# Token stage of a transformer layer in another order: keys turned in one go, query halves apart, values in 32 products

## The chip, the cores and the metric

The kernel runs on one core of one Trainium2 chip. The metric is the device time of one execution in microseconds; for a kernel several executions are timed and their median is given. Beside them one execution is profiled, and all rows of the trace come from that one.

## The reference, cut to what matters

Input `x` has 8192 rows (tokens) of 512 numbers. All is float32. The weights are drawn at random.

```
n   = layernorm(x)
cq, ckv = n @ Wc + bc, n @ Wckv + bckv               # 128 columns each
q   = [cq @ Wcq + bcq | cq @ Wqr + bqr]              # 16 heads of 32 + 16 columns
k   = [ckv @ Wck + bck | n @ Wkr + bkr]              # 16 heads of 32 + 16 columns
v   = ckv @ Wv + bv                                  # 16 heads of 32 columns
s   = q[token] @ k[token].T * scale                  # 16 x 16 for each token: heads against heads
x1  = x + layernorm(softmax(s) @ v -> 512 columns, @ Wo + bo)
xf  = layernorm(x1)
out = x1 + layernorm(experts(xf) + shared_mlp(xf))   # 64 experts, 6 chosen for a token
```

The attention is inside a token: its 16 heads attend to each other. So for 128 tokens there are 128 little products of 16 x 48 x 16 (scores) and of 16 x 16 x 32 (values).

## The kernel before, in words

The kernel has two stages, one after the other. The first, `token_pipeline`, goes through 64 tiles of 128 tokens and does everything up to the hidden layer of the shared MLP and the choice of experts. The second, `experts_and_norm`, runs the 64 experts, adds the results to the rows and normalises. Only the first is touched.

The token stage is a software pipeline written out by hand. Each engine has a function `iteration(i, par)`; in iteration `i` tile `i` is at its first step (latents), tile `i-1` gets queries, keys and values, `i-2` its scores, probabilities and value products, `i-3` the product with `wo` and the first residual, `i-4` the second layernorm's statistics, `i-5` the shared MLP's first product and the gate, `i-6` its stores. The order of work on an engine is the order of the `if active(...)` blocks in its function; engines wait for each other by counting semaphores, and a wait stops all that stands behind it on the same engine. The middle iterations run in a loop on all engines, two iterations in one turn of the loop.

The order of TensorE in one iteration: transposes of `xf` into `s0` (half of the score banks), transposes of the queries (`turn(q, ...)`) into banks b3 and b7, the first part of the latents' product into b5 (`high`, 8 matmuls of 512 columns), transposes of half of the keys into b2, the second part of the latents (`low`, 4 matmuls), transposes of the other half of the keys into b3, `v` into b6, the two query halves into b4 and b5, the first half of the MLP's product (`wgu`, 12 matmuls of 416 columns) into b7, scores, transposes of `oin`, the second half of `wgu` into b4, `high` of `wo` into b7, transposes of the first half of the probabilities, `low` of `wo`, transposes of the second half, key product `wck` into b6, transposes of the latents, `rank` (one small product, L611), and the value products (L623) into b4 and b5.

Every float32 product of dense weights is split in three: high part by high part and high part by low part (`high`, L502/L503 and L473/L474), and low part by high part (`low`, L508 and L477). ScalarE (ACT) writes the high parts, VectorE (DVE) subtracts to make the low parts (`low_part`, L767). Small products (scores, values) are plain float32; a plain float32 matmul appears in the trace as two MATMUL instructions.

Scores and values go by blocks of four tokens. `spread` on ACT copies the transposed queries and keys out of PSUM, 48 partitions x 256 elements at a time, 8 copies for queries and 8 for keys (L644, tiles qT and kT), into 64-row halves of qT and kT. The scores are then 32 products with 48 rows and 64 columns of weights, and 64 moving columns. For the values, `vbd` holds the values of a tile with (half, token of the block, head) on the partitions, and the value step makes for each of 8 column blocks four products: two halves of the partitions (64 rows) times two column groups, each with 32 moving columns:

```
last = nc.tensor.matmul(pv_ps[h][64 * g:64 * g + 64, n * DH:n * DH + DH],
                        probT[64 * h:64 * h + 64, n, 64 * g:64 * g + 64],
                        vbd[64 * h:64 * h + 64, par, 2 * n + g], start=True, stop=True)
```

The two partition halves go to two banks (`pv_ps`: halves of b4 and b5), and DVE scales each bank into `o` (L904). `o` then travels through memory to change its layout: SP (the DMA queue's engine) stores it with four DMAs to `o_scratch` and, when those have landed, loads it back with four DMAs into `oin`, which TensorE transposes about half an iteration later. `v` goes through `v_scratch` into `vbd` in the same manner.

DVE's order in an iteration: statistics of x (`st<-xin`), low part of `xfT`, statistics of x1, `lat` and the rotary part of `k` (L817, L821, both read b5), `v` (L827), the two query halves (L832), `xf` (L762), the gated unit's first half (L776 to L783, after ACT's tanh L682), the softmax steps (L845 to L858), low part of `oT`, gate steps, the gated unit's second half, sums, `y` (L891), `k` (L894), statistics of y, `o` (L904, twice), low parts of `latT` and `xT`, `yn`.

Ahead of the pipeline the weights are loaded in parts, staged in tiles that the pipeline does not use yet (wo's four parts in `vbd`), and split (`split`) on ACT and DVE in iterations -1, 0 and 1.

Of the kernel before, what the change touches and what calls it, by code (L numbers as in the profile page):

```python
# [35 lines left out]
ALU = mybir.AluOpType  # L36
# [71 lines left out]
def settle(eng):  # L108

    eng.nop(nofuse=True)  # L110
# [47 lines left out]
def token_pipeline(nc, x, xt, cst, w_lat, b_lat, w_q, b_q, w_ck, b_ck, w_v, b_v, w_o, b_o, w_gu,  # L158
                   x1_d, xf_d, h_d, acc_d, v_d, o_d, rank_d, wlat, wq, wck, wv, load_expert, c, tri, all_ranks, ranks_in):
    ctx = ExitStack()  # L160
    with ctx:
# [14 lines left out]
        pv_ps = (b4[:, 0:256], b5[:, 0:256])  # L176
# [21 lines left out]
        v_all = sb("vbd", [P, 4 * D])  # L198
        vbd = v_all[:, 0:2 * D].rearrange("p (a n d) -> p a n d", a=2, d=DH)
# [22 lines left out]
        rstd = [sb(f"rstd{n}", [P, 1 if n else 2]) for n in range(3)]  # L222
        smax4 = sb("smax4", [P, NBLK, B4])
# [19 lines left out]
        vs = v_all[:]  # L243
# [14 lines left out]
        latent_bias_in = sem("latent_bias_in")  # L258
# [39 lines left out]
        a_kT = count("a_kT", 8)  # L298
# [19 lines left out]
        d_pv = count("d_pv", 2)  # L318
# [33 lines left out]
        def _(sp):  # L352
# [6 lines left out]
            for n, (stage, _, _, src) in enumerate(parts):  # L359
                if n in SPLIT_BEFORE:  # L360
                    sp.wait_ge(part_lo, SPLIT_BEFORE[n])
                sp.dma_start(stage, src).then_inc(part_in[n], 16)
                if n == KD - 1:
                    sp.dma_start(blat[:], b_lat.partition_broadcast(P)).then_inc(latent_bias_in, 16)
                    load_x(1, 1)
# [5 lines left out]
            def iteration(i, par):  # L371
# [54 lines left out]
                if isinstance(i, int) and i == 1:  # L426
                    sp.wait_ge(part_lo, KD + 3 + KD)
                if active(i - 1):
# [8 lines left out]
                    for b in range(2):  # L437
                        sp.dma_start(vbd[64 * b:64 * b + 64, 1 - par], src[b]).then_inc(v_in[1 - par].sem, 16)
# [21 lines left out]
        def _(pe):  # L460
# [57 lines left out]
            def iteration(i, par):  # L518
                latents = b5, [xT[:, :, n, :] for n in range(KD)], [wlat[:, :, n, :] for n in range(KD)]
                normed = [xfT[:, :, n, :] for n in range(KD)]  # L520
# [36 lines left out]
                if active(i - 1):  # L557
                    pe.wait_ge(d_pv.sem, d_pv.at(i - 3))
                    for n, b in enumerate((b4, b5)):
                        if n == 1:  # L560
                            pe.wait_ge(d_lat.sem, d_lat.at(i))
                        product(b[:, 0:8 * DQ], [latT[:, 1 - par, :, 0, :]], [wq[:, :, 0, n * 8 * DQ:(n + 1) * 8 * DQ]],
                                d_latT, i - 1, pe_q)
                if active(i - 5):
# [11 lines left out]
                if active(i - 3):  # L576
                    pe.wait_ge(o_in.sem, o_in.at(i - 3))
                    pe.wait_ge(a_kT.sem, a_kT.at(i - 2))
                    transposes(b3, [oin[:, n * P:(n + 1) * P] for n in range(KD)], pe_oT)
# [18 lines left out]
                if active(i - 2):  # L598
                    pe.wait_ge(a_exp.sem, a_exp.at(i - 2, 2))
                    transposes(s1, [pr[:, n * P:(n + 1) * P] for n in range(4, 8)], pe_pT)  # L600
# [3 lines left out]
                if active(i):  # L604
                    pe.wait_ge(d_lat.sem, d_lat.at(i))
                    pe.wait_ge(a_kT.sem, a_kT.at(i - 2, 4))
                    transposes(b2, [lat[:, n * P:(n + 1) * P] for n in range(2)], pe_latT)
                if active(i - 5):
# [4 lines left out]
                if active(i - 2):  # L613
                    pe.wait_ge(a_pT.sem, a_pT.at(i - 2))
                    pe.wait_ge(d_q.sem, d_q.at(i - 1))
                    pe.wait_ge(d_h.sem, d_h.at(i - 5))
                    pe.wait_ge(v_in[par].sem, v_in[par].at(i - 2))
                    settle(pe)
                    for n in range(8):
                        for b in range(2):  # L620
                            for g in range(2):
                                h = (b + g) % 2
                                last = nc.tensor.matmul(pv_ps[h][64 * g:64 * g + 64, n * DH:n * DH + DH],  # L623
                                                        probT[64 * h:64 * h + 64, n, 64 * g:64 * g + 64],
                                                        vbd[64 * h:64 * h + 64, par, 2 * n + g],
                                                        start=True, stop=True)
                    last.then_inc(pe_pv.sem, 1)
# [4 lines left out]
        def _(act):  # L632
# [13 lines left out]
            def iteration(i, par):  # L646
                def spread(dst, src, done, n):

                    for a in range(2):
# [22 lines left out]
                if active(i - 2):  # L672
                    act.wait_ge(pe_kT.sem, pe_kT.at(i - 2, 1))
                    by_token = kT.rearrange("p (c t) (m a) -> p a m c t", t=B4, a=2)
# [54 lines left out]
        def _(dve):  # L729
# [59 lines left out]

            def iteration(i, par):  # L790
# [6 lines left out]
                if active(i - 4):  # L797
                    dve.wait_ge(g_x1.sem, g_x1.at(i - 4))
                    stats(2, x1[:], i - 4)
# [651 lines left out]
```

## Time and profile before

| | us |
|---|---|
| median of 3 runs | 1968.72 (1955.16 to 1973.68) |
| profiled execution, its own time | 1969.8 |
| its span, first to last instruction | 1967.8 |
| PE busy in the span | 1804.6 (92%) |
| DVE busy | 1458.7 (74%) |
| ACT busy | 1039.1 (53%) |
| POOL busy | 548.1 (28%) |

The span is the time between the first and the last instruction of the core; the execution's own time is a little longer. PE is TensorE's matmul side, PEld its weight loads, which run beside the matmuls. A busy share over the whole span mixes the token stage (to about 1,290 us) with the expert stage. Times of a row are the start from the span's start and the duration; the difference of two starts on one engine is what an instruction costs in a packed stream, since consecutive instructions overlap.

### The profile page before, as it was taken

The numbers are of one execution on the slowest core, as the hardware profiler recorded it, in microseconds if no ns is written. First come the engines' busy times: TensorE is split into PE (matmuls) and PEld (weight loads), VectorE is DVE, ScalarE is ACT, GpSimd is POOL, SyncE is SP. The second block draws the span as 40 slices with busy tenths as digits, with TensorE's granted clock in tenths as the row PEclk, the third lists the DMA queues.
The fourth block names the chain that finished last, engine by engine and source line by source line (L and its number), as shares of the span: only waits on it lengthen the run. The fifth ranks groups of instructions, "written<-read, shape, count | busy, mean of one in ns | idle before, by whom it ended". The sixth has DMA issues, their size and how long they took to land. (4 is left out here: it accounts for less than half of the span.)

```text
span 1967.8 us, 53720 instructions
## 1 busy us (share of the span) xinstructions
PE 1804.6 (92%) x16329; PEld 1410.4 (72%) x16329; DVE 1458.7 (74%) x3876; ACT 1039.1 (53%) x2257; POOL 548.1 (28%) x772
## 2 busy tenths in 40 slices
PE   5899999999999999999999999966799999978886
PEld 3688888888888888888888888753455555556564
DVE  6688888888888888888888888844344444439897
ACT  4576667676767676766666666621233323223333
POOL 1021212121212121212121212111344444437777
PEclk8799999999999999999999999977899999999999
DMA  6355565656565656565566656476999999979994
GB/s 221 82 146 161 151 170 149 170 149 171 148 170 148 169 149 170 153 165 154 165 154 164 163 156 171 119 191 222 293 306 307 288 293 299 290 233 387 403 385 162
DMA packets 549277, 400.85 MB, mean 204 GB/s; under 512 B 424873, under 2 KB 433193, under 8 KB 549161
## 3 DMA queue, kind: packets, MB, share of 16 engines
q1 hardware_dynamic: 528672, 341.77, 59.3%
q0 software_dynamic: 14336, 35.66, 7.7%
q10 hardware_dynamic: 6208, 22.68, 3.1%
q8 instruction: 30, 0.49, 0.1%
q14 instruction: 31, 0.25, 0.0%
HBM read 249.24 MB, written 150.63 MB: 203 GB/s over the span
## 5 line engine op out<-in xcount | busy, mean ns | idle before, releaser
L935 POOL TENSOR_SCALAR ve<-mv 128x1 f32<-128x1 f32 x192 | 43.1, 225 | 986.1 <-DVE mv L758 986.1
L644 ACT COPY kT<-bank 48x256 f32<-48x256 f32 x512 | 307.9, 601 | 12.6
L1140 PE MATMUL e_gu<-w,xgT 128*128 128x384 f32 x512 | 187.3, 510 | 20.7 <-issue 11.1
L473 PE MATMUL bank<-wgu,xfT 128*128 128x416 f32 x512 | 188.9, 369 | 6.5 <-ACT xfT L644 5.6
L644 ACT COPY qT<-bank 48x256 f32<-48x256 f32 x512 | 187.7, 367 | 12.6 <-PE bank L466 1.6
L474 PE MATMUL bank<-wgu,xfT 128*128 128x416 f32 x512 | 182.8, 357 | 0.0
L1301 DVE SCALAR_TENSOR_TENSOR tanh<-tanh,e_gu 128x192 f32<-128x192 f32 x64 | 22.6, 354 | 174.9 <-ACT tanh L1227 174.9
L1140 PEld LDWEIGHTS e_gu<-w,xgT 128*128 128x128 f32 x512 | 94.2, 194 | 80.3 <-issue 20.3
L1384 POOL DMA_INDIRECT acc_scratch<-eo,sidx x64 | 101.5, 1586 | 128.8 <-ACT eo L1223 112.0
L644 ACT COPY probT<-score_ps 128x512 f32<-128x512 f32 x128 | 75.2, 588 | 112.0 <-PE score_ps L466 112.0
L1163 PE MATMUL e_ps<-w,hidT 96*128 96x512 f32 x256 | 127.0, 618 | 1.6 <-ACT hidT L1215 0.9
L776 DVE SCALAR_TENSOR_TENSOR th<-th,bank 128x176 f32<-128x176 f32 (+1 forms) x128 | 44.7, 349 | 108.2 <-ACT th L682 105.5
L477 PE MATMUL bank<-wgu,xfT 128*128 128x416 f32 x512 | 118.1, 353 | 0.0
L502 PE MATMUL bank<-wlat,xT 128*128 128x512 f32 x256 | 108.2, 423 | 6.4 <-DVE wlat L749 5.0
L937 POOL TENSOR_TENSOR rstd<-ve,mhalf 128x1 f32<-128x1 f32 x192 | 108.8, 566 | 16.0
L1215 ACT COPY hidT<-e_ps 96x256 f32<-96x256 f32 x64 | 23.5, 367 | 167.7 <-PE e_ps L1147 167.7
L950 POOL TENSOR_TENSOR x<-yn,xres 128x512 f32<-128x512 f32 x64 | 82.3, 1285 | 91.5 <-DVE yn L762 91.5
L1244 ACT ACTIVATE f_acc<-f_acc,f_shift,f_rstd 128x512 f32<-128x512 f32 x64 | 48.7, 808 | 107.1 <-POOL f_shift L1405 107.1
L473 PEld LDWEIGHTS bank<-wgu,xfT 128*128 128x128 f32 x512 | 98.9, 193 | 8.3 <-ACT xfT L644 6.4
L1413 POOL TENSOR_TENSOR f_res<-f_acc,f_res 128x512 f32<-128x512 f32 x64 | 94.6, 1500 | 33.9 <-ACT f_acc L1244 18.2
L502 PE MATMUL bank<-wo,oT 128*128 128x512 f32 x256 | 102.7, 401 | 1.4 <-ACT oT L644 1.4
L503 PE MATMUL bank<-wlat,xT 128*128 128x512 f32 x256 | 103.2, 403 | 0.0
(178 smaller groups left out, 4789.2 us busy)
## 6 DMA issues: line engine op xcount, KB each, us to landing
w<-w_eg SPq DMA_DIRECT2D x60, 768.0 KB, 6.5
acc_scratch<-zero SPq DMA_DIRECT2D x130, 256.0 KB, 4.0
w<-w_ed SPq DMA_DIRECT2D x60, 384.0 KB, 10.5
xf_scratch<-xf SPq DMA_DIRECT2D x64, 288.0 KB, 2.1
xin<-x SPq DMA_DIRECT2D x64, 256.0 KB, 3.0
x_raw<-xt SPq DMA_DIRECT2D x64, 256.0 KB, 3.3
v_scratch<-v SPq DMA_DIRECT2D x64, 256.0 KB, 3.5
vbd<-v_scratch SPq DMA_DIRECT2D x128, 128.0 KB, 3.2
```

What stands on the lines that cost most here:

```text
L473: nc.tensor.matmul(dst, a[:, 0], b[:, 0], start=(n == 0), stop=False)
L474: nc.tensor.matmul(dst, a[:, 0], b[:, 1], start=False, stop=False)
L477: last = nc.tensor.matmul(dst, a[:, 1], b[:, 0], start=False, stop=(n == len(lhs) - 1))
L502: nc.tensor.matmul(dst, a[:, 0], b[:, 0], start=(n == 0), stop=False)
L503: nc.tensor.matmul(dst, a[:, 0], b[:, 1], start=False, stop=False)
L644: nc.scalar.copy(dst, src).then_inc(done.sem, 1)
L937: nc.gpsimd.tensor_tensor(to, ve[n][:], mhalf[:], ALU.pow).then_inc(g_rstd[n].sem, 1)
L950: nc.gpsimd.tensor_tensor(x1[:], yn[:], xres[:], ALU.add).then_inc(g_x1.sem, 1)
L1140: last = nc.tensor.matmul(gu_ps[par], xgT[:, par, n, :], w1[:, place, n, :], start=(n == 0), stop=(n == KD - 1))
L1163: last = nc.tensor.matmul(out_ps, hidT[:, n, :], w2[0:PI, (place - 1) % NW, n, :], start=(n == 0), stop=(n == 1))
L1384: nc.gpsimd.indirect_dma_start(acc_d[1 - par], bass.IndirectOffsetOnAxis(sidx[:, (place - 1) % NW, :].bitcast(U32), 0), eo[:, (place - 1) ...
L1413: nc.gpsimd.tensor_tensor(r, acc[:, u, n * D:(n + 1) * D], r, ALU.add).then_inc(g_sum.sem, 1)
```

## The change

It reorders the token stage on TensorE and DVE and changes three steps. Nothing of the arithmetic's result changes.

1. TensorE: `low` of the latents stands right behind `high`, and both halves of the keys are transposed one after the other behind it. `high` no longer waits for `o` of the tile before (`d_pv`), because b5 no longer holds value products.
2. TensorE: the second query half (into b5) moves from in front of `wgu`'s first half to behind it, with its wait for `d_lat`. DVE's matching add moves behind the gated unit's first half.
3. TensorE: both halves of the probabilities are transposed one after the other, inside wo's product; `low` of `wo` comes behind them.
4. Values: `vbd` is block diagonal: for each token block and partition half b, the values fill column part b and zeros the other. One product has 128 rows, 64 columns of weights and 64 moving columns; 16 products (32 MATMUL instructions) take the place of 32 (64). All go to b4, and DVE makes `o` in one operation. The zeros are written once, by a memset on GpSimd in iteration 0, behind the split of wo's parts; the DMAs into `vbd` write strided pieces of 32 numbers. The value products stand ahead of `rank`.
5. Keys: ACT makes 6 of the 8 key copies (b3's second partition half is left out), DVE makes the other two (`d_kT`), behind the first query half.
6. DVE: `lat` and the rotary part of `k` move ahead of the statistics of x1 (and, in iteration 0, ahead of the weight splits), `k` moves behind `o`.
7. The latent bias is counted with the other biases: DVE waits for all five in iteration 0.

```
 TensorE
                 if active(i):
                     pe.wait_ge(a_xT.sem, a_xT.at(i))
                     pe.wait_ge(d_q.sem, d_q.at(i - 2))
-                    pe.wait_ge(d_pv.sem, d_pv.at(i - 3))
                     high(*latents)
+                if active(i):
+                    pe.wait_ge(d_xT.sem, d_xT.at(i))
+                    low(*latents, pe_lat)
                 if active(i - 2):
...
                     turn(k[:, par], pe_kT, 0, b2)
-                if active(i):
-                    pe.wait_ge(d_xT.sem, d_xT.at(i))
-                    low(*latents, pe_lat)
                 if active(i - 2):
                     pe.wait_ge(a_qT.sem, a_qT.at(i - 2, 4))
                     turn(k[:, par], pe_kT, 1, b3)
...
                 if active(i - 1):
                     pe.wait_ge(d_pv.sem, d_pv.at(i - 3))
-                    for n, b in enumerate((b4, b5)):
-                        if n == 1:
-                            pe.wait_ge(d_lat.sem, d_lat.at(i))
-                        product(b[:, 0:8 * DQ], ...)
+                    queries(0, b4)
                 if active(i - 5):
...
                     product(b7[:, 0:GU], normed, [wgu[:, :, n, 0:GU] for n in range(KD)], d_xfT, i - 5, pe_gu)
+                if active(i - 1):
+                    pe.wait_ge(d_lat.sem, d_lat.at(i))
+                    queries(1, b5)
                 if active(i - 2):
                     pe.wait_ge(a_kT.sem, a_kT.at(i - 2))
+                    pe.wait_ge(d_kT.sem, d_kT.at(i - 2))
...
                     transposes(s0, [pr[:, n * P:(n + 1) * P] for n in range(4)], pe_pT)
+                if active(i - 2):
+                    pe.wait_ge(a_exp.sem, a_exp.at(i - 2, 2))
+                    transposes(s1, [pr[:, n * P:(n + 1) * P] for n in range(4, 8)], pe_pT)
                 if active(i - 3):
                     pe.wait_ge(d_oT.sem, d_oT.at(i - 3))
                     low(*turned, pe_wo)
...
                     for n in range(8):
-                        for b in range(2):
-                            for g in range(2):
...
+                        for g in range(2):
+                            last = nc.tensor.matmul(b4[64 * g:64 * g + 64, n * 64:n * 64 + 64],
+                                                    probT[:, n, 64 * g:64 * g + 64],
+                                                    vbd[:, par, 2 * n + g].rearrange("p b d -> p (b d)"),
+                                                    start=True, stop=True)
                     last.then_inc(pe_pv.sem, 1)
+                if active(i - 5):
+                    pe.wait_ge(d_r.sem, d_r.at(i - 5, 6))
+                    pe.wait_ge(a_pT.sem, a_pT.at(i - 2))
+                    nc.tensor.matmul(rank_ps, chosen[:], tri[:], start=True, stop=True).then_inc(pe_rank.sem, 1)
 ACT
-                    spread(by_token, b3, a_kT, 1)
+                    spread(by_token, b3, a_kT, 1, (0,))
 DVE (behind the first query half)
+                if active(i - 2):
+                    dve.wait_ge(pe_kT.sem, pe_kT.at(i - 2))
+                    dve.wait_ge(pe_s.sem, pe_s.at(i - 3))
+                    settle(dve)
+                    sv = b3[64:64 + DQ, :].rearrange("p (m r c t) -> p r m c t", m=4, r=2, t=B4)
+                    for half in range(2):
+                        nc.vector.tensor_copy(by_token[64 * half:64 * half + DQ, 1, 4:8], sv[:, half]).then_inc(d_kT.sem, 1)
...
                     nc.vector.tensor_tensor(o[:].rearrange("p (n d) -> p n d", d=DH),
                                             b4[:].rearrange("p (n d) -> p n d", d=DH),
                                             srec[:].unsqueeze(2).broadcast_to([P, NBLK, DH]), ALU.mult).then_inc(d_pv.sem, 1)
 SP
-                        sp.dma_start(vbd[64 * b:64 * b + 64, 1 - par], src[b]).then_inc(v_in[1 - par].sem, 16)
+                        sp.dma_start(vbd[64 * b:64 * b + 64, 1 - par, :, b, :], src[b]).then_inc(v_in[1 - par].sem, 16)
 GpSimd
+                if isinstance(i, int) and i == 0:
+                    pool.wait_ge(part_lo, 11)
+                    nc.gpsimd.memset(vbd[:], 0.0).then_inc(zeroed, 1)
```

## Rows read from the trace of the kernel before

**Rows 1.** The page: busy us, then 40 equal slices in tenths, span.

```profile
PE 1804.6 (92%) x16329; PEld 1410.4 (72%) x16329; DVE 1458.7 (74%) x3876; ACT 1039.1 (53%) x2257; POOL 548.1 (28%) x772
PEclk8799999999999999999999999977899999999999
```

**Rows 2.** Stretch 102 to 1243: us, busy by engine, clock, DMA share, GB/s.

```profile
102.00:1243.00 1141.00, 1118.52 (x12946) 968.98 (x12944) 974.04 (x2497) 760.50 (x1686) 209.26 (x407) 1.00 0.60 159
```

**Rows 3.** Tile `lat`, same stretch: duration ns min/median/max, first and last start.

```profile
L817 DVE SCALAR_TENSOR_TENSOR lat<-bank,rstd,blat x59: 482/483/485, 102.4 to 1242.1; 128x256 f32<-128x256 f32 x59
```

**Rows 4.** Waits, same stretch: who for whom, total us, times, longest us.

```profile
DVE th L776 <- ACT th L682: 95.0, 58, 1.7
...
PEld score_ps L493 <- issue: 21.2, 58, 0.6
PEld bank L473 <- DVE k L821: 17.8, 49, 1.4
...
PEld bank L623 <- issue: 11.0, 54, 0.3
...
PEld bank L466 <- DMA oin<-o_scratch: 6.7, 16, 1.2
```

**Rows 5.** Timeline of PE, 726 to 739: start, duration, line, operation.

```profile
726.77 1.14 PE L623 MATMUL bank<-vbd,probT 64*64 64x32 f32 x64
727.84 0.66 PE L466 MATMUL score_ps<-c,xf 128*128 128x128 f32 x4
...
729.16 0.47 PE L502 MATMUL bank<-wlat,xT 128*128 128x512 f32 x1
729.47 0.40 PE L503 MATMUL bank<-wlat,xT 128*128 128x512 f32 x1
729.70 0.39 PE L502 MATMUL bank<-wlat,xT 128*128 128x512 f32 x1
...
731.10 0.60 PE L466 MATMUL bank<-c,k 128*128 128x128 f32 x4
...
732.47 0.60 PE L466 MATMUL bank<-c,k 128*128 128x128 f32 x4
...
737.28 1.16 PE L493 MATMUL score_ps<-kT,qT 48*64 48x64 f32 x64
738.39 0.66 PE L466 MATMUL bank<-c,oin 128*128 128x128 f32 x4
```

**Rows 6.** Timeline of ACT, same iteration.

```profile
732.14 4.99 ACT L644 COPY kT<-bank 48x256 f32<-48x256 f32 x8
```

**Rows 7.** Groups by shape, 102 to 1243: count, busy us, mean ns, idle before.

```profile
L644 ACT COPY kT<-bank 48x256 f32<-48x256 f32 x468 | 281.8, 602 | 11.5
L644 ACT COPY qT<-bank 48x256 f32<-48x256 f32 x464 | 170.1, 367 | 10.0
```

**Rows 8.** Timeline of DVE, same iteration.

```profile
728.26 0.75 DVE L904 TENSOR_TENSOR o<-bank,srec 128x256 f32<-128x256 f32 x2
...
735.57 0.54 DVE L762 TENSOR_SCALAR xf<-x,mv,rstd 128x512 f32<-128x512 f32 x1
737.71 0.34 DVE L776 SCALAR_TENSOR_TENSOR th<-th,bank 128x176 f32<-128x176 f32 x1 [1.59 <-ACT th L682]
...
745.84 0.68 DVE L894 TENSOR_TENSOR k<-bank,bck 128x512 f32<-128x512 f32 x1
```

**Rows 9.** Timeline of SP's DMA issues, same iteration.

```profile
729.12 2.63 SPq L379 DMA_DIRECT2D o_scratch<-o  x4
...
733.43 2.59 SPq L394 DMA_DIRECT2D oin<-o_scratch  x4
```

**Rows 10.** Tile `oin`, 100 to 1236: from issue to landing.

```profile
DMA to landing us min/median/max: 2.2/2.6/4.2
```

**Rows 11.** Timeline of the start, 17 to 25 us, all engines.

```profile
18.67 0.93 DVE L749 TENSOR_TENSOR wq<-kT,wq 128x768 fp32r<-128x768 f32 x1
...
21.47 1.62 PE L508 MATMUL bank<-wlat,xT 128*128 128x512 f32 x4
...
25.00 0.47 DVE L817 SCALAR_TENSOR_TENSOR lat<-bank,rstd,blat 128x256 f32<-128x256 f32 x1
```

More of the change, by code:

```diff
@@ L297, in token_pipeline @@
         a_qT = count("a_qT", 8)
-        a_kT = count("a_kT", 8)
+        a_kT = count("a_kT", 6)
+        d_kT = count("d_kT", 2)
         a_exp = count("a_exp", 2)
@@ L317, in token_pipeline @@
         d_s = count("d_s", 9)
-        d_pv = count("d_pv", 2)
+        d_pv = count("d_pv")
         d_h = count("d_h", 4)
@@ L519, in iteration, with queries @@
                 latents = b5, [xT[:, :, n, :] for n in range(KD)], [wlat[:, :, n, :] for n in range(KD)]
+                def queries(n, b):
+                    product(b[:, 0:8 * DQ], [latT[:, 1 - par, :, 0, :]], [wq[:, :, 0, n * 8 * DQ:(n + 1) * 8 * DQ]],
+                            d_latT, i - 1, pe_q)
                 normed = [xfT[:, :, n, :] for n in range(KD)]
@@ L607, in iteration @@
                     transposes(b2, [lat[:, n * P:(n + 1) * P] for n in range(2)], pe_latT)
+                if active(i - 2):
+                    pe.wait_ge(a_pT.sem, a_pT.at(i - 2))
+                    pe.wait_ge(d_q.sem, d_q.at(i - 1, 1))
+                    pe.wait_ge(d_h.sem, d_h.at(i - 5))
+                    pe.wait_ge(v_in[par].sem, v_in[par].at(i - 2))
+                    settle(pe)
+                    for n in range(8):
+                        for g in range(2):
[3 more added lines that the diff above has]
+                                                    start=True, stop=True)
+                    last.then_inc(pe_pv.sem, 1)
                 if active(i - 5):
@@ L646, in iteration, with spread @@
             def iteration(i, par):
-                def spread(dst, src, done, n):
-                    for a in range(2):
+                def spread(dst, src, done, n, pair=range(2)):
+                    for a in pair:
                         sv = src[64 * a:64 * a + DQ, :].rearrange("p (m r c t) -> p r m c t", m=4, r=2, t=B4)
@@ L788, in low_x, with queries @@
                 low_part(xT, x_raw[:, 1 - par, :], d_xT)
+            def queries(i, n, b):
+                dve.wait_ge(pe_qT.sem, pe_qT.at(i - 2))
+                dve.wait_ge(pe_q.sem, pe_q.at(i - 1, n + 1))
+                nc.vector.tensor_tensor(q[:, 8 * n:8 * n + 8, 0:DQ], b[:, 0:8 * DQ].rearrange("p (h d) -> p h d", d=DQ),
+                                        bq[:, n * 8 * DQ:(n + 1) * 8 * DQ].rearrange("p (h d) -> p h d", d=DQ),
+                                        ALU.add).then_inc(d_q.sem, 1)
             def iteration(i, par):
@@ L796, in iteration @@
                     low_part(xfT, s0, d_xfT)
[L797 to L806 removed]
                 if isinstance(i, int) and i == 0:
[L808 to L810 removed]
+                    dve.wait_ge(biases_in, 16 * 5)
                 if active(i):
@@ L823, in iteration @@
                                                    ALU.mult, ALU.add).then_inc(d_lat.sem, 1)
+                if active(i - 4):
+                    dve.wait_ge(g_x1.sem, g_x1.at(i - 4))
+                    stats(2, x1[:], i - 4)
+                if isinstance(i, int) and i == -1:
+                    low_x(i, par)
+                    dve.wait_ge(centred, 1)
+                    for n in range(KD):
+                        nc.vector.tensor_tensor(parts[n][0], parts[n][0], b2, ALU.subtract).then_inc(centred, 1)
+                if isinstance(i, int) and i in PART_AT:
+                    split(i)
                 if active(i - 1):
@@ L840, in iteration @@
                     gated(i, par, 0, b7)
+                if active(i - 1):
+                    queries(i, 1, b5)
                 sp4 = score_ps[:].rearrange("p (n t h) -> p n t h", n=NBLK, t=B4)
-                half = [slice(n * NBLK // 2, (n + 1) * NBLK // 2) for n in range(2)]
+                halves = [slice(n * NBLK // 2, (n + 1) * NBLK // 2) for n in range(2)]
                 if active(i - 2):
                     dve.wait_ge(pe_s.sem, pe_s.at(i - 2))
-                    nc.vector.tensor_reduce(smax4[:, half[0]], sp4[:, half[0]], AX.X, ALU.max).then_inc(d_s.sem, 1)
-                    nc.vector.tensor_reduce(smax4[:, half[1]], sp4[:, half[1]], AX.X, ALU.max).then_inc(d_s.sem, 1)
+                    nc.vector.tensor_reduce(smax4[:, halves[0]], sp4[:, halves[0]], AX.X, ALU.max).then_inc(d_s.sem, 1)
+                    nc.vector.tensor_reduce(smax4[:, halves[1]], sp4[:, halves[1]], AX.X, ALU.max).then_inc(d_s.sem, 1)
                     dve.wait_ge(d_s.sem, d_s.at(i - 2, 2))
@@ L857, in iteration @@
                     for n in range(2):
[L858 to L859 removed]
+                        nc.vector.tensor_tensor(prob[:, halves[n]], sp4[:, halves[n]],
+                                                sref[:, halves[n]].unsqueeze(3).broadcast_to([P, NBLK // 2, B4, H]),
                                                 ALU.subtract).then_inc(d_s.sem, 1)
```

69 lines of the change are left out of this document (15 added, 54 removed).

## The prediction

> **What bounds the kernel now.** The page comes first: PE is busy 92% of the span, and its clock is granted in full in nearly every slice between the start and the expert stage [rows 1]. Only the token stage is changed, so the next view is the table by stretches over the even part of it, 102 to 1243 us: PE busy 1118.5 of 1141 us (98%), clock 1.00, DVE 974.0 (85%), ACT 760.5 (67%) [rows 2]. TensorE's stream sets the pace, at full clock; the reader should note DVE's 85%, since the change gives DVE more to do. How long is an iteration? `lat` is made once in each: 59 of them from 102.4 to 1242.1, so 1139.7/58 = 19.65 us [rows 3]. PE being nearly always busy, a gain must come out of packed instructions or out of the small holes. The waits list the holes [rows 4], per iteration: 21.2/58 = 0.37 before the scores, 17.8/58 = 0.31 before the second query half (released by DVE's rotary part of `k`, L821), 0.19 before the values, and 6.7/58 = 0.12 before the transposes of `oin`, where a DMA came late 16 times in 58. DVE itself stands 95.0/58 = 1.64 us waiting for ACT's tanh L682; no other hole of its has that size.
>
> **The change part by part, per iteration.** Prices on PE are differences of starts, since neighbours overlap.
>
> Second query half behind `wgu`: the wait on L821 goes. It is 0.31 us of the weight loads' idle time, some of which a running matmul covers; I take 0.25. What is late next there? `wgu`'s first half now starts about 0.8 us earlier, and needs ACT's query copies, finished when the key copies start at 732.14, while `wgu` would start about 4.9 us after the first key transposes, at 734.0 [rows 5, 6]: no wait.
>
> Start of the scores: the eight key copies on ACT run from 732.14 for 4.99 us to 737.13, and the scores start at 737.28 [rows 5, 6]. So ACT's chain ends exactly where the scores begin. The hole of 0.37 has a part that any change of product kind with several waits seems to cost (0.19 before the values, rows 4); the rest, 0.18, is put down to ACT, and I take 0.15 as gained. With six copies of 0.60 [rows 7] ACT needs 3.7 us. It starts later, since the first keys are turned only behind `low`: that is 4 x 0.23 us + 0.08 behind today's start at 731.10, so 732.1, and ready some 0.6 later at 732.7 [rows 5]; 732.7 + 3.7 = 736.4, against scores that would start at about 736.8. Covered, by 0.4 us.
>
> Merging transposes: after transposes, the first wide product costs 729.47 - 729.16 = 0.31 us where the next costs 729.70 - 729.47 = 0.23 [rows 5]. Each return from transposes to a product costs 0.08; the keys in one go and the probabilities in one go save one each: 0.16. The cost would be that the second half of the probabilities is wanted 0.95 us earlier (4 x 0.23 of `low`). It was 1 us and more ready before PE came; I count nothing, and it is the thinnest of the covers on this side.
>
> Values: 64 MATMULs of 32 columns take 727.84 - 726.77 = 1.07 us, 16.7 ns each. 64 of 64 columns in four tiles (the scores) take 738.39 - 737.28 = 1.11, 17.3 each [rows 5]. Twice the columns cost the same, so it looks like a rate of instructions and not of columns. Now 32 MATMULs of 64 columns with all 128 rows, hence two tiles in place of four. Low end: 32 x 17.3 ns = 0.55 us, if the rate of instructions stays. High end with both column groups at work: each group's pass keeps the 4 x 17.3 = 69 ns that a tile has now, 16 passes: 1.11. If the column groups did not overlap at all: 32 x 69 ns = 2.2. No row has this shape; I take the middle of the first two, 0.85, and gain 0.22. The Trainium skill (TensorEngine Tiling (Array Packing), Available Configurations) lists 64x64 as four tiles and 128x64 as two. By that rule the products lose in tiles what they save in number, the values stay at about 1.1 us, and the iteration saves 0.25 us less; the trace shows only the four-tile form.
>
> `high` without `d_pv`, `rank` behind the values: no row has a wait on the one, and the other is the same instruction elsewhere. Nothing. SP's strided DMA pieces are 128 bytes on the memory side before and after; nothing.
>
> Sum on PE: 0.25 + 0.15 + 0.16 + 0.22 = 0.78, iteration 19.65 - 0.78 = 18.87 us.
>
> **DVE, the engine that receives work.** Its sequence, without the wait for the tanh, fills 19.65 - 1.64 = 18.0 us. Added: two copies of 256 elements. Nearest below is half of `o`, same size out of PSUM, 0.75/2 = 0.38 [rows 8]; above it, ACT pays 0.602 for the scattered key copies where the same count of elements costs 0.367 for queries [rows 7], and by that ratio DVE would pay 0.62. I take 0.42, since DVE's row is the nearer one: 0.84. `o` in one operation should be like `k` (0.68 for 512 elements, rows 8) in place of 0.75: -0.07. Sum 18.0 + 0.84 - 0.07 = 18.8, at the ends 18.7 and 19.2. So DVE's chain comes level with PE. What hides the copies is the hole between `xf` (735.57 + 0.54 = 736.11) and 737.71 [rows 8]: 1.6 us, of which the earlier tanh (about 0.8 us) takes half. The copies stand in front of the gated unit and so of the softmax, with the scores waiting for them on PE. They can start when `v` and the first query half are done, about 1.4 us before 736; both would be over at about 736.4, before the scores at 736.8. `lat` earlier gives the rotary part of `k` a wait for the second key transposes of some 0.3 us, with `v` and all else queued behind it. `k` behind `o` is a loss to nobody: its reader is the next iteration's key transposes, over 4 us later. I charge nothing to PE for these, and keep the ends for the range.
>
> **Start.** DVE's weight splits begin at 18.67 and run packed until `lat` at 25.00, while `low` of the first latents ends at 21.47 + 1.62 = 23.09 [rows 11]. Now `lat` stands ahead of the splits: DVE is idle from 18.67 to 23.1, and the same splits end 4.4 us later, with the low parts of the next tile behind them. I add 4.4 us once. GpSimd's memset has its next user, SP's load of the values, some 10 us later: nothing. The expert stage is not touched.
>
> **The forecast.** About 60 iterations at the steady pace x 0.78 = 46.8 us saved, 4.4 lost: 42.4. From the profiled execution, 1969.8 - 42.4 = 1927 us; that execution is 1.1 us above the median of 1968.72, which changes nothing. With the values at 0.55 the gain is 18 us more (1909), at 1.11 it is 16 less (1943). 1% is 20 us, about what a measurement here can tell from no change.
>
> **The rivals.**
>
> A, DVE becomes the bound. For it: 18.8 of 18.9 us, with `prob`, exp and the transposes in a chain behind it. Against it: DVE has its hole just where the copies go. With copies of 0.62 and the 0.3 us wait, an iteration is about 19.2 to 19.3; saved 0.4 x 60 = 24, less 4.4: 1950.
>
> B, the round trip of `o` through memory decides. Its stores are issued from 729.12 on, its loads end their issue at 733.43 + 2.59 = 736.02, a load lands 2.2 to 4.2 us after its issue [rows 9, 10]; the last, issued at about 735.4, lands at 738.0 by the median, and `oin` is wanted at 738.39. Today 16 of 58 come late. A trip that takes the same time with an iteration's transposes wanted 0.4 us earlier is late most of the time, at 0.3 to 0.4 us each. Against it: `o` is also earlier against the start of the next iteration, since `rank` now follows the values and `k` follows `o`. Saved 0.45 x 60 - 4.4: about 1947.
>
> C, slower: the two column groups of the value products do not overlap. Then the step costs 2.2 us, 1.1 more than now, the iteration 18.87 + 1.35 = 20.2, and 60 x 0.57 + 4.4 = 39 us are lost: 2008. It decides once the step costs over 1.6 us. Against it: in the scores the same column groups at 64 rows evidently run beside each other, for 64 passes of 69 ns would need 4.4 us.
>
> D, the holes only move: the scores wait for DVE's copies as long as they did for ACT's, the probabilities' second transposes wait for the exponential, and the values stay at 1.1. Left are the 0.16 of the merges and some 0.05: 60 x 0.2 - 4.4 = 8 us, 1962.
>
> **How the numbers follow.** Forecast 0.60 (1909 to 1945), A 0.14 and B 0.11 (1940 to 1958), C 0.07, D 0.08. The predicted time is 1927. The range leaves out C and the slow half of D above, and below it reaches the cheap values with a little more of the holes closed: 1900 to 1962. Faster by over 1% (below 1949): the forecast and somewhat over half of A and B, 0.75. Slower by over 1%: C, and a little for a start that costs more, 0.08. Within 1%: 0.17.
>
> **What would show it.** `lat` every 18.9 us at full clock; no hole before the second query half; the value products at 0.55 to 1.1 us from their start to the next operation's; two DVE copies of 0.4 us into kT and DVE's wait for the tanh nearly gone; the first `lat` at about 23 us and the second about 4 us later than before. I am wrong if the waits show PE standing for `oin`, for DVE's kT copies or for the exponential by more than 0.3 us an iteration, or if the value products take over 1.6 us.

## The result and the profile after

The changed kernel takes 1948.2 us (median of 18 runs, 1930.5 to 1957.8) against 1966.8 us for the kernel before (18 runs, 1955.2 to 1975.8): ratio 0.9906, interval 0.9885 to 0.9927. It is faster by 18.6 us; the forecast was 42.4, with a range of 1900 to 1962. The time lies inside the range, but the gain is 0.44 of the one forecast, and 1948 is rival A's 1950 almost to the number. In two of the later runs single executions took far longer than the rest (one of e9 4173 us, two of e10 2519 and 2915 us); every number below leaves them out.

Where did the time go in the traces? `lat`, made once an iteration, divides the profiled run in three. From the sixth `lat` to the last there are 58 iterations: 1242.05 - 102.36 = 1139.7 us before, 1218.88 - 100.13 = 1118.8 us after. That is 19.65 and 19.29 us an iteration, 20.9 us in all. The first six cost 2.2 us less, and behind the last `lat` (end of the token stage and all of the expert stage) 718.9 us stand against 725.8. Those 6.9 us are not the change's: in the runs of this study that last part took from 710 to 734 us, with the code of the expert stage the same in all.

The page of the changed kernel, busy time by engine, then the table by stretches for the same stretch as [rows 2]:

```profile
PE 1780.3 (92%) x14281; PEld 1411.3 (73%) x14281; DVE 1537.3 (79%) x3940; ACT 965.5 (50%) x2129; POOL 547.9 (28%) x773
```
```profile
102.00:1243.00 1141.00, 1115.36 (x11337) 987.94 (x11335) 1067.61 (x2602) 705.62 (x1597) 212.20 (x411) 1.00 0.61 162
```

The clock is still 1.00. PE is as busy as before and DVE rose from 85% to 94% of the stretch. A PE at 98% looks like the bound in both kernels; which engine waits for the other has to come out of the waits, and for the changed kernel they read like this (answering to [rows 4]):

```profile
PEld score_ps L492 <- issue: 35.5, 60, 1.6
...
PE score_ps L492 <- issue: 17.6, 30, 1.3
DVE mv L759 <- DVE st L755: 16.7, 81, 0.2
...
PEld bank L465 <- DMA oin<-o_scratch: 5.9, 11, 1.5
...
DVE o L908 <- PE bank L620: 1.8, 5, 0.4
DVE y L900 <- PE bank L507: 1.0, 2, 0.7
```

Before, DVE stood 95.0 us for the tanh. That line is gone, and nothing is in its place: DVE waits 1.8 and 1.0 us for other engines in 60 iterations. The hole before the second query half is gone too. The hole before the scores grew from 21.2 to 35.5 us of PEld's time, 0.6 us an iteration. From PE's last query matmul to the first of the scores it is 0.63 us by the mean of 59 iterations, and 0.27 in e3 below, where nothing holds the scores. One iteration of DVE shows why (answering to [rows 8]; the same columns):

```profile
701.28 0.47 DVE L817 SCALAR_TENSOR_TENSOR k<-bank,rstd,blat 128x256 f32<-128x256 f32 x1
701.67 0.69 DVE L755 BATCH_NORM_STATS2 st<-x 128x6 f32<-128x512 f32 x1
...
702.71 0.69 DVE L833 TENSOR_TENSOR v<-bank,bv 128x512 f32<-128x512 f32 x1
703.31 0.55 DVE L794 TENSOR_TENSOR q<-bank,bq 128x384 f32<-128x384 f32 x1
703.89 1.22 DVE L842 COPY kT<-bank 48x256 f32<-48x256 f32 x2
705.14 0.55 DVE L763 TENSOR_SCALAR xf<-x,mv,rstd 128x512 f32<-128x512 f32 x1
705.72 0.34 DVE L777 SCALAR_TENSOR_TENSOR th<-th,bank 128x176 f32<-128x176 f32 x1
...
715.42 0.69 DVE L908 TENSOR_TENSOR o<-bank,srec 128x512 f32<-128x512 f32 x1
...
720.35 0.48 DVE L817 SCALAR_TENSOR_TENSOR k<-bank,rstd,blat 128x256 f32<-128x256 f32 x1
```

and PE in the same iteration (answering to [rows 5]):

```profile
704.45 0.34 PE L476 MATMUL bank<-wq,latT 128*128 128x384 f32 x1
705.41 1.16 PE L492 MATMUL score_ps<-kT,qT 48*64 48x64 f32 x64 [0.62 <-issue]
...
713.89 1.15 PE L620 MATMUL bank<-vbd,probT 128*64 128x64 f32 x32
714.87 0.22 PE L628 MATMUL score_ps<-tri,chosen 128*64 128x128 bf16 x1
715.02 0.66 PE L465 MATMUL score_ps<-c,xf 128*128 128x128 f32 x4
...
719.19 1.04 PE L465 MATMUL bank<-c,k 128*128 128x128 f32 x8
```

The key copies take 1.22 us. They end at 705.11 and the scores start at 705.41, while PE had issued its last query matmul at 704.45. The list calls the hole "issue", for no single semaphore event shows as its end; the next section shows whose it is. Now follow the time from one rotary part of `k` (701.28) to the next (720.35), 19.07 us. DVE: 3.83 to the end of the copies. Then 0.30 to the scores. PE: 9.61 from the scores (705.41) to the next `xf` transposes (715.02), 4.17 to the key transposes (719.19), and 1.16 until DVE, which needs all of them, starts L817. That is a closed cycle through two engines, and it is as long as the iteration; its loosest link is L817, which starts 0.43 behind `lat` here and 0.40 by the median, where DVE alone needs 0.39: in this kernel the key transposes hold it little or not at all. DVE alone, packed from end to end, is a second one of the same length. (It is the shorter of the two iterations in a turn of the loop; the other has some 0.3 us at the loop's end.) So the candidates are: DVE's total (theory 1), the cycle over the key transposes and copies (theory 2), and the round trip of `o` (theory 3, rival B).

### The profile page after: what moved, and what is told of

It is laid out like the page before. It is cut to its first block and busy times, and to the rows that moved or that the text cites. A ratio compares the mean times of both kernels' runs of the same rounds, so it can differ in the third digit from the quotient of the medians.

```text
span 1937.8 us, 49723 instructions
## 1 busy us (share of the span) xinstructions
PE 1780.3 (92%) x14281; PEld 1411.3 (73%) x14281; DVE 1537.3 (79%) x3940; ACT 965.5 (50%) x2129; POOL 547.9 (28%) x773
## 5 line engine op out<-in xcount | busy, mean ns | idle before, releaser
L942 POOL TENSOR_SCALAR ve<-mv 128x1 f32<-128x1 f32 x192 | 42.1, 219 | 920.2 <-DVE mv L759 920.2
L646 ACT COPY kT<-bank 48x256 f32<-48x256 f32 x384 | 231.1, 602 | 37.5 <-PE bank L465 29.5
L646 ACT CAST oT<-bank 128x512 fp32r<-128x512 f32 x64 | 37.5, 586 | 157.8 <-PE bank L465 157.8
L1423 POOL TENSOR_TENSOR f_res<-f_acc,f_res 128x512 f32<-128x512 f32 x64 | 95.1, 1507 | 33.5 <-ACT f_acc L1254 17.8
L501 PE MATMUL bank<-wo,oT 128*128 128x512 f32 x256 | 102.7, 401 | 1.3 <-ACT oT L646 1.3
L502 PE MATMUL bank<-wo,oT 128*128 128x512 f32 x256 | 102.3, 400 | 0.0
```

The source lines that it names most:

```text
L501: nc.tensor.matmul(dst, a[:, 0], b[:, 0], start=(n == 0), stop=False)
L502: nc.tensor.matmul(dst, a[:, 0], b[:, 1], start=False, stop=False)
L646: nc.scalar.copy(dst, src).then_inc(done.sem, 1)
L1423: nc.gpsimd.tensor_tensor(r, acc[:, u, n * D:(n + 1) * D], r, ALU.add).then_inc(g_sum.sem, 1)
```

## The experiments

All ratios are to runs of the kernel before on the same chip (medians 1962.9 to 1967.2 us in the experiments). "Iteration" is from the sixth to the last `lat` over 58, as above, and so leaves out the expert stage; but it comes from one profiled execution of each kernel. Sixty times its difference to the kernel before agrees with the measured gain to 7 us in every run, so a difference of under 0.1 us an iteration needs the waits beside it to be believed.

| run | edit | iteration us | median us | ratio to before, interval |
|---|---|---|---|---|
| before | | 19.65 | 1966.8 | |
| changed | | 19.29 | 1948.2 | 0.9906 (0.9885 to 0.9927) |
| e1 | changed, low part of xT on GpSimd | 19.22 | 1940.5 | 0.9874 (0.9841 to 0.9907) |
| e2 | before, low part of xT on GpSimd | 19.88 | 1981.4 | 1.0075 (1.0047 to 1.0102) |
| e3 | changed, key copies early | 19.25 | 1948.9 | 0.9908 (0.9875 to 0.9942) |
| e4 | changed, all key copies on ACT | 19.65 | 1973.5 | 1.0032 (1.0004 to 1.0059) |
| e5 | changed, short sum | 19.14 | 1933.9 | 0.9853 (0.9800 to 0.9906) |
| e6 | changed, short sum and key copies early | 18.94 | 1925.9 | 0.9806 (0.9759 to 0.9854) |
| e7 | changed, seven copies on ACT, keys apart | 18.91 | 1921.2 | 0.9781 (0.9743 to 0.9819) |
| e8 | changed, dense key copies | 18.98 | 1927.4 | 0.9811 (0.9766 to 0.9855) |
| e9 | before, values in 32 products | 19.53 | 1956.7 | 0.9947 (0.9923 to 0.9972) |
| e10 | before, two key copies on DVE | 19.50 | 1959.0 | 0.9966 (0.9949 to 0.9983) |
| e11 | changed, seven copies on ACT, keys together | 19.12 | 1939.1 | 0.9864 (0.9843 to 0.9886) |

**e1 and e2: the low part of xT on GpSimd.**

```
 DVE
-                if active(i + 1) and (not isinstance(i, int) or i >= 0):
-                    low_x(i, par)
 GpSimd, behind root(1, ...)
+                if active(i + 1):
+                    pool.wait_ge(a_xT.sem, a_xT.at(i + 1))
+                    settle(pool)
+                    nc.gpsimd.tensor_tensor(xT[:, 1]..., x_raw[:, 1 - par, :], xT[:, 0]..., ALU.subtract).then_inc(d_xT.sem, 1)
```

> The changed kernel with one thing moved: the low part of xT (0.60 us of DVE an iteration) is made by GpSimd. Theory 1 (DVE's total bounds the changed kernel: its instructions fill 19.2 us of an iteration of 19.2, PE's alone would fill 18.8): the iteration falls to 18.85 to 18.95 us, PE becomes the bound again, the kernel comes to about 1926 us (ratio to before 0.98). Theory 2 (the bound is only where DVE's key copies stand in its order, so that the scores wait for them): they would come 0.6 us earlier too, so the same fall of the iteration is expected; this run alone doesn't tell the two apart. Theory 3 (the round trip of o through memory sets the pace): no gain, since o is made no earlier against the transposes of oin; the wait before those grows.

> The same move in the kernel before. Theory 1: DVE has 1.6 us of slack there, so nothing changes: iteration 19.6 to 19.7 us, ratio 0.995 to 1.005; DVE's wait for the tanh grows by 0.6 us. If off-loading DVE as such helps whatever the bound, 0.3 us or more are gained here too (ratio 0.99).

Neither came as theory 1 had it: e1 gained 0.06 us in place of 0.35, and e2 lost 0.23 where nothing was expected. Both have the same main reason, and the timelines of e1, GpSimd and then DVE, show it:

```profile
713.66 1.30 POOL L956 TENSOR_TENSOR xT<-x_raw,xT 128x512 fp32r<-128x512 f32 x1
```
```profile
714.25 1.00 DVE L763 TENSOR_SCALAR yn<-y,mv,rstd 128x512 f32<-128x512 f32 x1
...
717.08 0.47 DVE L813 SCALAR_TENSOR_TENSOR lat<-bank,rstd,blat 128x256 f32<-128x256 f32 x1
717.60 0.48 DVE L817 SCALAR_TENSOR_TENSOR k<-bank,rstd,blat 128x256 f32<-128x256 f32 x1
```

`yn` runs while GpSimd works on its 512 columns, and takes 1.00 us; in the changed kernel it takes 0.54 (mean of 59: 542 ns; in e1 970 ns over 56). So 0.43 of the 0.60 us taken off DVE came back. In e1 the rest goes as theory 2 says: L817 starts 0.52 us behind `lat` here (0.50 by the median) where 0.39 is its own pace; DVE is early and stands for the key transposes. In e2 `yn` starts just behind GpSimd's subtraction and takes still longer:

```profile
711.35 1.29 POOL L946 TENSOR_TENSOR xT<-x_raw,xT 128x512 fp32r<-128x512 f32 x1
711.49 1.43 DVE L762 TENSOR_SCALAR yn<-y,mv,rstd 128x512 f32<-128x512 f32 x1
```

Its mean is 1425 ns over 55 iterations against 540 in the kernel before: 0.89 us more, where 0.60 were taken off. DVE's slack of 1.6 us lies in front of the tanh; between the tanh and the rotary part of `k` (L820) it has next to none, so 0.29 us more there reaches PE. PE's weight loads wait 42.1 us for L820 in 55 iterations, where it was 17.8 in 49 before, and the iteration is 0.23 us longer. So e2 says nothing against theory 1; what was moved came back larger.

**e3, e5 and e6: the two cycles cut one at a time, and together.** In e3 the block of the two copies stands ahead of `stats(2, ...)`. In e5 the row sum of the probabilities reads one head in place of 16, so 15 of 16 terms are left out; e6 is both edits.

```
-  nc.vector.tensor_reduce(ssum[:], prob[:].rearrange("p n t h -> p n (t h)"), AX.X, ALU.add)
+  nc.vector.tensor_reduce(ssum[:], prob[:, :, :, 0], AX.X, ALU.add)
```

> The changed kernel with DVE's two key copies ahead of the statistics of x1 (and so of v and the first query half) in place of behind them: the copies end about 2 us earlier. Theory 1: the hole before the scores goes or moves, but the iteration stays 19.2 to 19.3 us, ratio to before 0.99. Theory 2: scores start 0.5 us earlier and the iteration falls to 18.8 us, ratio 0.98.

> The changed kernel with DVE's row sum of the probabilities cut from 1024 elements to 64 (one head of 16; that part of the sum is left out). It takes about 1.0 us off DVE behind the scores, on nobody's path. Theory 1 (DVE's total is the only bound): iteration 18.85 us, ratio to before 0.975. Theory 2 (a second cycle is as long: key transposes on PE, then DVE's rotary part of k, statistics of x1, v, first query half and key copies from 5.3 to 9.2 us of the iteration, then scores and the rest of PE's stream): nothing is shortened there, iteration 19.15 to 19.25 us, ratio 0.985 to 0.991, and DVE is seen to wait for the key transposes.

> The short sum and the early key copies together (part of the sum left out). Theory 1: as the short sum alone, 18.85 us. Theory 2: only this cuts both cycles: 18.85 us, ratio 0.975, while each alone stays at 19.2. Theory 3 (the round trip of o through memory is right behind): PE waits for oin in most iterations, 0.3 us or more, and the iteration stays above 19.1 us.

e3: the hole before the scores went from 35.5 to 15.6 us, and the iteration stayed (19.25). The wait list of e3 has the next one in the queue:

```profile
PEld bank L465 <- DMA oin<-o_scratch: 23.9, 43, 1.7
```

PE runs ahead to the transposes of `oin` and stands there, because `o` comes when DVE makes it. e5: DVE has slack, in the waits of e5 for PE,

```profile
DVE o L908 <- PE bank L620: 20.8, 57, 0.4
DVE y L900 <- PE bank L507: 18.4, 55, 1.5
...
PEld bank L465 <- DMA oin<-o_scratch: 2.1, 3, 1.3
```

0.7 us an iteration, and still the iteration is 19.14: theory 1 alone had 18.85. It is 0.15 us less than 19.29, so by this reading the cycle of theory 2 was the shorter of the two by about that much; the ratios of e3 and e5 do not stand clear of the changed kernel's (0.9885 to 0.9927), that of e6 does. e6, with both edits, comes to 18.94, though each alone is worth 0.15 and 0.04. That is the sign of two bounds of nearly one length. In e6 the waits for `oin` are 5.7 us in 11 cases, about as in the changed kernel (5.9 in 11): theory 3's round trip is no bound of its own at this pace; in e3 it only passed DVE's lateness on.

**e8: what the copy costs.** DVE's two copies write densely, beside the key tile; the scores then read old keys in that quarter.

```
-  nc.vector.tensor_copy(by_token[64 * half:64 * half + DQ, 1, 4:8], sv[:, half])
+  nc.vector.tensor_copy(kside[64 * half:64 * half + DQ].rearrange("p (m c t) -> p m c t", m=4, t=B4), sv[:, half])
```

> The changed kernel with DVE's two key copies written densely beside the key tile (the scores then read stale keys in that quarter). If the scattered write is what makes a copy cost 0.62 us, they fall to 0.38 each: 0.48 us less on DVE and on the cycle over the copies, iteration 18.85 us, ratio 0.975. If reading out of PSUM with a stride costs it, they stay at 0.6 and the iteration at 19.25 us.

The groups by shape, of the changed kernel and of e8:

```profile
L842 DVE COPY kT<-bank 48x256 f32<-48x256 f32 x120 | 72.1, 601 | 3.8
```
```profile
L843 DVE COPY kT<-bank 48x256 f32<-48x256 f32 x114 | 48.7, 427 | 3.6
```

The read is the same in both. The scattered write costs 0.17 us a copy, and without it the iteration falls to 18.98. That is the experiment nearest to the forecast: with copies of 0.43 us, where the forecast had 0.42, 0.67 of the 0.78 us forecast are there.

**e4, e11 and e7: who copies the keys, and when ACT may begin.** e4 gives ACT all eight copies; e11 seven and DVE one; e7 is e11 with `low` of the latents again between the two halves of the keys. The edit of e11 and e7 (ACT copies its share of the contested partitions first, and DVE waits for that):

```
 ACT
+                    sv = b3[64:64 + DQ, :].rearrange("p (m r c t) -> p r m c t", m=4, r=2, t=B4)
+                    copy(by_token[0:DQ, 1, 4:8], sv[:, 0], a_kT)
                     spread(by_token, b3, a_kT, 1, (0,))
 DVE
+                    dve.wait_ge(a_kT.sem, a_kT.at(i - 2, 5))
...
-                    for half in range(2):
-                        nc.vector.tensor_copy(by_token[64 * half:64 * half + DQ, 1, 4:8], sv[:, half]).then_inc(d_kT.sem, 1)
+                    nc.vector.tensor_copy(by_token[64:64 + DQ, 1, 4:8], sv[:, 1]).then_inc(d_kT.sem, 1)
 TensorE (e7 only)
-                    low(*latents, pe_lat)         # behind high
                     turn(k[:, par], pe_kT, 0, b2)
+                    low(*latents, pe_lat)         # behind the first half of the keys
```

> The changed kernel with all eight key copies on ACT again. Theory 1: DVE has slack again (18.0 us), but ACT's eight copies begin only when the first keys are turned, 4.8 us into the iteration, and end at 9.8; the scores start 0.9 us later than PE could: iteration about 19.6 us, ratio 0.995 to 1.005. So the move of two copies to DVE is a condition of turning the keys in one go. If ACT's chain does not matter, 18.85 us and ratio 0.98.

> The kernel with one key copy on DVE and seven on ACT, but the keys turned in one go as in the change. ACT starts its copies at 4.8 us and ends at 9.17, so the scores start at about 9.4 where PE could at 9.05: iteration 19.1 us, ratio 0.985. If ACT's start does not matter, 18.85 us, ratio 0.976, better than with the keys turned apart.

> A candidate for the better kernel, complete: ACT makes seven key copies, DVE one, and the keys are turned apart again (first half between high and low of the latents), so that ACT starts its copies 0.5 us earlier and ends at 8.7 us. DVE loses 0.62 us, the cycle over the key copies loses 0.62 too, PE's stream gains 0.08. Theories 1 and 2 both: iteration 18.9 to 18.95 us, ratio 0.976. Theory 3: PE waits for oin instead, 19.15 us.

In e4 DVE has its slack back (95.0 us of waiting for the tanh in 56 iterations, as before) and the whole gain is gone, 19.65. With eight copies ACT ends 9.8 us into the iteration (counted here and below from the transposes of `xf`) and the scores start at 9.9. The keys turned in one go start ACT's chain 0.5 us later: in the changed kernel ACT waits for the first key transposes 27.6 us in 58 iterations, a wait that the kernel before does not have. e11 needs 19.12, e7 18.91. The timeline of ACT in e7 has no hole between query and key copies, and ACT is through 8.7 us into the iteration by the median, 0.45 before the scores start at 9.14; in e11 it ends at 9.17 and the scores start at 9.33:

```profile
704.25 3.11 ACT L646 COPY qT<-bank 48x256 f32<-48x256 f32 x8
707.38 4.37 ACT L646 COPY kT<-bank 48x256 f32<-48x256 f32 x7
711.88 0.32 ACT L685 ACTIVATE th<-bank 128x176 f32<-128x176 f32 x1
```

e7 computes all of the reference and is faster than both kernels: 1921.2 us, 0.9781 (0.9743 to 0.9819), an interval wholly below the changed kernel's. It keeps the values, the query halves and the probabilities of the change, turns the keys apart, and leaves DVE one key copy of eight.

**e9 and e10: two parts of the change alone, on the kernel before.**

> The kernel before with the values alone in the new form (32 MATMULs, block-diagonal values, one operation for o, no wait of the latents on o). Both theories of the loss: PE is the bound there, so the iteration falls by what the step costs less, 1.07 - 0.98 = 0.09 us, and by up to 0.1 more for the wait on o; 19.5 us, ratio 0.991 to 0.996. If the block-diagonal form cost something elsewhere (strided writes of the DMAs, zeros), the ratio is 1.00 or more.

> The kernel before with the two key copies on DVE alone, behind both query halves (and the biases counted together at the start). There DVE has 1.6 us of slack at that place and the two copies cost 1.24; the scores waited for ACT's last copy. If slack alone counts: PE gains the 0.15 us before the scores, iteration 19.5 us, ratio 0.992. If the copies' place behind the rotary part of k, v and the queries makes them end later than ACT's eight would (5.9 + 0.4 + 0.6 + 0.9 + 1.24 = 9.2 us against 9.3), no gain: 19.6 us, ratio 0.997 to 1.002.

The edits are those of the change's points 4 (with `high`'s wait on `d_pv` left out, and `rank` still ahead of the values) and 5 (with 7, and the copies behind both query halves). The values gave 0.12 us an iteration: the step went from a mean of 1.18 us to 1.08. The key copies on DVE gave 0.15: the hole before the scores is 15.3 us in 55 iterations where it was 21.2 in 58, 0.09 us each; the waits for `oin` fell from 6.7 to 2.7 us, 0.07 each; and the hole before the second query half stayed (18.7 in 51). That is a gain of the size of the holes on PE, with DVE's slack paying.

## Why the prediction was wrong

The step that failed is the one headed "DVE, the engine that receives work", and in it the price of the copies: "I take 0.42, since DVE's row is the nearer one: 0.84". They cost 601 ns each, 1.24 us for both, the upper end of the range given there (0.62). With it the prediction's own sum reads 18.0 + 1.24 - 0.07 = 19.2 us, against 19.29 measured, and with dense copies of 0.43 us the iteration is 18.98 (e8). The choice went by engine where the write pattern decided: `o` writes pieces of 32 numbers in a row, the key tile takes single numbers 16 apart. ACT's two rows had shown it, 602 ns for the keys and 367 for the queries, which go out in pieces of four; e8 shows it for DVE (427 ns dense).

The second part of the step that failed is "I charge nothing to PE for these". The prediction saw the 0.3 us wait for the key transposes and all that is queued behind it, and took the copies to end at 736.4, which is 8.6 us into the iteration; their median end is 9.1 and the mean 9.3, and the scores start 9.5 us in by the mean, where PE could start them at 9.14 (in e3, where nothing holds them, they follow the last query matmul by 0.27 us; here, 705.41 - 704.45 = 0.96). Of the lateness of the copies 0.4 us is their price. Their start was nearly right: 7.7 us into the iteration by the 736.4 less 0.84, and 7.9 by the median. (The prediction's "about 1.4 us before 736" does not fit its own 736.4: 734.6 is where the queries begin, and with the first half of them done it is 735.1.)

```profile
734.64 1.01 DVE L832 TENSOR_TENSOR q<-bank,bq 128x384 f32<-128x384 f32 x2
```

Rival A was this mechanism (copies of 0.62 and the wait) with 19.2 to 19.3 us and 1950 us; it had 0.14. What it called a saturated DVE was that and one thing more: the cycle through the key transposes, as e5 and e6 show. No engine's busy share shows such a cycle.

Point by point:

- Second query half: right. The wait for the rotary part of `k` (L821, now L817) is gone from the list, and PE comes to the scores with no hole earlier in its stream.
- Start of the scores: ACT's chain was as computed (first copy 4.8 us into the iteration, forecast 4.86; six copies over at 8.5). But DVE's copies took its place at the same gate. The 0.15 was not gained but turned into 0.6 of waiting; part of rival D.
- Merging transposes: wrong, 0.16 us forecast and nothing gained. `high`, keys, `low` and `v` take 4.46 us together where they took 4.45, and the probabilities, `low` of `wo` and `wck` 2.50 as before (means, start to start). The first wide product is 0.08 cheaper each time, as forecast: `low` of the latents takes 719.19 - 718.26 = 0.93 where it took 1.02. But eight transposes in one go take 719.99 - 719.19 = 0.80, and the two fours took 0.35 each. The trace of the kernel before had the row, the eight query transposes at a mean of 0.80:

```profile
728.33 1.04 PE L466 MATMUL bank<-c,q 128*128 128x128 f32 x8
```

 The thin cover of the second probabilities held. And the merge of the keys starts ACT's key copies later, which was named but counted as covered; e4 and e11 show what it costs once ACT has seven or eight of them.
- Values: 714.87 - 713.89 = 0.98 us, between the ends 0.55 and 1.11, taken as 0.85. The rule of the Trainium skill weighed there (TensorEngine Tiling (Array Packing), Available Configurations: four tiles of 64x64, two of 128x64) would give 1.1, and the row lies halfway between it and the value taken. Each of 32 instructions costs 30.7 ns, against 16.7 of the 64 before: it is neither purely a rate of instructions nor of tiles. Rival C did not come.
- `rank`, counted at nothing, got cheaper: it takes 0.14 to 0.30 us behind the values, a mean of 0.20 against 0.33 ahead of them. The values' mean fell from 1.18 to 0.98, so both together gave 0.33 us where 0.22 was forecast.
- The sum on PE, 18.87 us, was nearly right as what PE alone needs: e6 and e7 run at 18.94 and 18.91. But part of that is luck: in e6 the merges gave nothing, values and `rank` 0.33, and the queries with the hole before the scores 0.38 (forecast 0.25 + 0.15), 0.71 in all.
- The start: 4.4 us forecast. DVE indeed stood still, 4.74 us, and not for the latents but for the last bias:

```profile
22.86 0.48 DVE L813 SCALAR_TENSOR_TENSOR lat<-bank,rstd,blat 128x256 f32<-128x256 f32 x1 [4.74 <-DMA bo<-b_o]
...
33.29 0.48 DVE L813 SCALAR_TENSOR_TENSOR lat<-bank,rstd,blat 128x256 f32<-128x256 f32 x1 [1.35 <-PE bank L507]
```

 The second `lat` came at 33.29 in place of 33.11, the third at 42.07 in place of 40.46. The splits ended 5 us later, but `high` of the second tile started 1.7 us earlier (25.86, before at 27.59) and took up most of it. The cost was 0.2 to 1.6 us.
- Rival B: not the bound. The waits for `oin` are 5.9 us in 11 cases (before 6.7 in 16), and grow much only in e3 (23.9 us in 43), where DVE paces `o`.

In sum: of the 0.78 us forecast an iteration 0.36 came, 60 x 0.36 = 22 us. Of the 0.42 that did not, 0.35 is DVE's copies and the cycle through them (19.29 against 18.94 in e6), and 0.07 is PE's own sum, where the missing merges outweigh what values and `rank` gave beyond the forecast. The measured 18.6 us agree with the 20.9 us of the traces' steady stretch within the spread of the runs.

## What to carry to other kernels

When a step moves to another engine, take its price from the row with the same access pattern, even if that row is of the old engine: the scattered write cost 0.60 us on both, the dense one 0.43 on DVE, and the one in pieces of four 0.37 on ACT. And when the sums of two engines come within 2% of each other, write down the cycles that pass through both (who releases whom, once around an iteration) before charging nothing; shortening one of two equal cycles gives almost nothing (0.04 and 0.15 us here), both together 0.35. A step that is merged on the bound engine can delay the start of a long chain elsewhere: here the keys in one go cost ACT 0.5 us of its start and gave PE nothing, and giving back that merge and one copy was worth 0.38 us an iteration. And a price for a merge has to come from a row of the merged step: 0.08 us less on the product behind it was 0.09 us more on the eight transposes.

## What the hardware showed that was not expected

GpSimd's elementwise work slows a DVE operation beside it: `yn`, a tensor-scalar of 512 columns from SBUF to SBUF, took 970 ns on average with GpSimd's subtraction beside it (e1) and 542 ns without (the changed kernel), and 1425 against 540 ns where it started 0.14 us behind the subtraction (e2). In both timelines shown it ends 0.28 to 0.29 us behind the subtraction, however early it starts: it looks held until GpSimd is done rather than slowed, though no run tests that. The statistics of x, which stand beside GpSimd's addition for x1 in e1, kept their 0.69 us. The 32 value instructions on 128 rows by 64 columns cost 30.7 ns each, 0.98 us, up to the start of `rank` behind them, and 33.8 ns (1.08 us) in e9, where the transposes of `xf` stand behind them; the 64 on 64 rows cost 16.7. Whether the array's half, the row count or the switch to the neighbour sets these was not tried. Eight transposes of 128 x 128 in one go between two wide products took 0.79 us up to the second product (keys and probabilities of the changed kernel), and four took 0.35 (the kernel before).
